# The merge of eight work queues in three causal attentions: from a greedy plan with a clock of its own to a written-out string for each

## What is computed

```python
# sublayer 6; sublayers 0 and 4 mask before the softmax instead
scores = jnp.einsum('bthd,bshd->bhts', q, k)
scores = scores * mask
attn = jax.nn.softmax(scores / T ** 0.5, axis=-1)
out = jnp.einsum('bhts,bshd->bthd', attn, v).reshape(B, T, H * Dh)
return out @ Wo
...
x = _layernorm(x + _L0_attn_ref(x, ...), axis=-1)      # 0, attention
x = _layernorm(x + _L0_ffn_ref(x, ...), axis=-1)       # 1, gated feed-forward
x = _layernorm(x + _L1_attn_ref(x, ...), axis=-1)      # 2, windowed attention
x = _layernorm(x + _L1_ffn_ref(x, ...), axis=-1)       # 3, mixture of experts
x = _layernorm(x + _L2_attn_ref(x, ...), axis=-1)      # 4, attention
x = _layernorm(x + _L2_ffn_ref(x, ...), axis=-1)       # 5, one matrix with binary weights
x = _layernorm(x + _L3_attn_ref(x, ...), axis=-1)      # 6, attention
x = _layernorm(x + _L3_ffn_ref(x, ...), axis=-1)       # 7, gated, ternary weights
```

## Time and profile before

| | us |
|---|---|
| runs: median of 3 (lowest to highest) | 1041.98 (1037.92 to 1046.48) |
| the profiled execution, its own time | 1044.26 |
| its span, first to last instruction | 1042.5 |
| TensorE busy | 972.7 (93%) |
| VectorE busy | 695.9 (67%) |
| ScalarE busy | 531.3 (51%) |
| GpSimd busy | 334.6 (32%) |
| mean granted TensorE clock | 0.984 |

### The profile page before, as it was taken

How to read it: one execution, slowest core, us unless ns; L and a number is a source line. 1 busy time by engine, 2 the same in 40 slices (tenths; PEclk the granted TensorE clock), 3 DMA queues, 4 the chain that set the end, 5 groups by cost and what they waited for, 6 DMA issues and landing times. The chain is left out here.

```text
span 1042.5 us, 16974 instructions
## 1 busy us (share of the span) xinstructions
PE 972.7 (93%) x6102; PEld 549.8 (53%) x6102; DVE 695.9 (67%) x1987; ACT 531.3 (51%) x1140; POOL 334.6 (32%) x465
## 2 busy tenths in 40 slices
PE   8999999989999999999999999999999988889896
PEld 3544454676454564443487544445555444445585
DVE  2677774686797987453223467777772778877587
ACT  4566665433879881121102456665544535665442
POOL 4211112233578871000001121112211256672452
PEclk9999999999999999999999899999999989999999
DMA  6000000100000200210000011000000000000001
GB/s 257 2 1 1 2 1 2 56 1 2 8 20 19 123 2 1 107 44 0 1 1 1 1 74 48 2 1 2 1 1 1 1 1 2 1 2 1 2 1 41
DMA packets 4823, 21.64 MB, mean 21 GB/s; under 512 B 489, under 2 KB 1769, under 8 KB 3844
## 3 DMA queue, kind: packets, MB, share of 16 engines
q1 hardware_dynamic: 4740, 20.55, 5.2%
HBM read 19.01 MB, written 1.05 MB: 19 GB/s over the span
## 5 line engine op out<-in xcount | busy, mean ns | idle before, releaser
L1000 ACT ACTIVATE PB<-pair 128x1024 f32<-128x1024 f32 (+3 forms) x288 | 223.2, 811 | 134.1 <-PE pair L1789 132.8
L1260 DVE CUSTOM_DVE_ANT_0 junk<-bank,cst 128x128 bf16<-128x128 f32 (+3 forms) x384 | 171.1, 488 | 106.4 <-PE bank L1773 104.4
L831 POOL TENSOR_SCALAR_AFFINE_SELECT PB<-PB 128x256 f32<-128x256 f32 x192 | 78.6, 412 | 308.1 <-ACT PB L1000 306.6
L1263 DVE TENSOR_REDUCE pmx<-bank 128x1 f32<-128x512 f32 x192 | 122.5, 685 | 40.9 <-PE bank L1773 40.2
L1773 PE MATMUL bank<-KO_r,QO_r 64*128 64x512 f32 (+3 forms) x576 | 139.7, 411 | 6.6 <-DVE pmx L1260 2.3
L1807 PE MATMUL pvb<-PB,V 128*32 128x512 f32 (+3 forms) x1152 | 122.7, 497 | 10.8 <-ACT PB L1000 8.8
L1785 PE MATMUL pair<-QO_r,KO_r 64*128 64x512 f32 (+3 forms) x576 | 114.7, 389 | 12.6 <-ACT PB L1000 10.8
L1773 PEld LDWEIGHTS bank<-KO_r,QO_r 64*128 64x128 f32 x576 | 72.1, 186 | 102.2 <-DVE pmx L1260 40.8
L837 POOL TENSOR_TENSOR parts_r<-y_f,parts_r 128x512 fp32r<-128x512 f32 x24 | 30.9, 1287 | 276.0 <-ACT parts_r L971 276.0
L1789 PE MATMUL pair<-ms,sel_r 64*128 64x512 f32 (+3 forms) x576 | 101.1, 344 | 0.0
L1071 ACT ACTIVATE KO<-pair,nm 128x128 f32<-128x128 f32 x256 | 90.1, 392 | 9.8 <-DVE nm L1487 9.4
(11 more groups left out here) (237 smaller groups left out, 1701.5 us busy)
## 6 DMA issues: line engine op xcount, KB each, us to landing
WF<-in_moe_gu SPq DMA_DIRECT2D x1, 3520.0 KB, 12.2
WF<-in_tern_w SPq DMA_DIRECT2D x1, 3072.0 KB, 10.6
WA<-in_w_att SPq DMA_DIRECT2D x2, 1024.0 KB, 10.5
V<-in_moe_d SPq DMA_DIRECT2D x1, 1792.0 KB, 7.4
xT<-in_xT SPq DMA_DIRECT2D x2, 512.0 KB, 5.9
WA<-in_w_att SPq DMA_DIRECT2D x2, 512.0 KB, 7.5
X<-in_x SPq DMA_DIRECT2D x1, 1024.0 KB, 10.8
A<-in_rope SPq DMA_DIRECT2D x1, 1024.0 KB, 4.8
```

Source lines behind the costliest of these rows:

```text
L831: pool.affine_select(p2, p2, pattern=[[0, 2], [1, P]], compare_op=ALU.is_ge, fill=0.0, base=0, channel_multiplier=-1).then_inc(causal, 1)
L1000: act.activation(pb[:, st % 2, 2 * i:2 * i + 2, 0:n], ps[:, :, 0:n], ACT.Exp, scale=scale)\
L1260: r_done(dve.tensor_tensor_reduce(junk[:, (r_used - 1) % 3, 0:n], ps[:, 0:n], tri[:, HALF - n:HALF], 1.0, LOWEST, ALU.add, ALU.max, accum_ ...
L1263: r_done(dve.tensor_reduce(to, ps[:, 0:n], AX.X, ALU.max))
```

## The change

The ranks, the `Clock` and all rules of what may start are taken out. For each of the three attentions a string gives the order in which the eight queues are popped. The queues, their inner order, the items and what each engine issues for an item stay the same, as do the waits. `acc` still follows a stage's last pv, and `norm` the last proj; the `weights` and `late` items go in behind the same items as before.

```diff
-LEAN = 600
-
-
-class Clock:
...
+ORDER = {
+    0: "BBBBBUBUUBUBUBUUBBUUBUBUBUBUTUBXUXUXUBUBUBUXPUXBUBUBPUXBUUBUBUTPUXXUXUBUPXXUAXUPUXXUPUBXUXUPUXXUPXUU"
...
 def attention_plan(s):
...
-    turns, accs, out, extra = [], [], [], []
...
-        now = [f for f in found if f[0] <= clock.pe + 30]
-        queue = min(now, key=lambda f: f[1])[2] if now else min(found, key=lambda f: f[:2])[2]
-        issue(queue.pop(0))
+    out = [("outT",)] + [("proj", k) for k in range(TH)] + [("new",)]
+    if SUBLAYERS[s + 1] == BIN:
+        out += [("bin", k) for k in range(TH)] + [("bin_new",)]
+    queues = {"B": operands(s, first, second), "U": [u for stage in units for u in stage],
+              "T": [("mT",) + stage for stage in STAGES], "X": [("exp",) + step + (i,) for step in STEPS for i in range(TWO)],
+              "P": [("pv",) + step for step in STEPS], "A": [("accT",) + stage for stage in STAGES], "O": out,
+              "E": [("suffix", t) for t in reversed(range(NT))] if s == LAST_ATT else []}
+    behind = {("pv", g, qh, TH * (qh + 1) - 1): ("acc", g, qh) for g, qh in STAGES}
+    behind.update({("proj", TH - 1): ("norm",), ("bin", TH - 1): ("bin_norm",)})
+    plan = []
+    for queue in ORDER[s]:
+        plan.append(queues[queue].pop(0))
+        if plan[-1] in behind:
+            plan.append(behind[plan[-1]])
```

More of the change, by code:

```diff
@@ L251, in attention_plan @@
[L251 to L332, removed]
@@ L394, in attention_plan @@
-    while build or units or exps or pvs or turns or accs or out:
-        while units and units[0][0] == "m":
-            issue(units.pop(0))
-        found = []
-        for rank, queue in ((-9000, turns), (-200, pvs), (-500, accs), (-400, out), (-300, extra), (None, exps),
-                            (None, units), (800, build)):
-            if queue:
-                at = ready(queue[0])
-                if at is not None:
-                    if rank is None:
-                        rank = (clock.act if queue is exps else clock.dve - LEAN) - max(clock.pe, at)
-                    found.append([at, rank, queue])
-        if build and found[-1][2] is build:
-            need = [x for x in wanted(units[0]) if x[0] == "s"] if units else []
-            late = [("v", pvs[0][3] // 2)] if all(("exp",) + pvs[0][1:] + (i,) in done for i in range(TWO)) else []
-            if any(x not in done for x in need + late):
-                found[-1][1] = -1000
-        now = [f for f in found if f[0] <= clock.pe + 30]
-        queue = min(now, key=lambda f: f[1])[2] if now else min(found, key=lambda f: f[:2])[2]
-        issue(queue.pop(0))
+    out = [("outT",)] + [("proj", k) for k in range(TH)] + [("new",)]
@@ L414, in attention_plan @@
+    behind = {("pv", g, qh, TH * (qh + 1) - 1): ("acc", g, qh) for g, qh in STAGES}
[5 more added lines that the diff above has]
+            plan.append(behind[plan[-1]])
+    assert not any(queues.values())
     if BIN in SUBLAYERS[s - 1:s]:
@@ L417, in attention_plan @@
     if s == 4:
-        for n, behind in ((0, ("norm",)), (1, ("new",)), (2, ("accT",) + STAGES[-2]), (3, ("weights", 2)),
-                          (4, ("accT",) + STAGES[-1])):
-            plan.insert(plan.index(behind) + 1, ("weights", n))
+        for n, item in ((0, ("norm",)), (1, ("new",)), (2, ("accT",) + STAGES[-2]), (3, ("weights", 2)),
+                        (4, ("accT",) + STAGES[-1])):
+            plan.insert(plan.index(item) + 1, ("weights", n))
     return plan
```

87 lines of the change are left out of this document (11 added, 76 removed).

## The result

The changed kernel takes 1024.40 us (median of 4 runs, 1021.98 to 1031.87); the kernel before, beside it, 1044.23. The ratio is 0.9842, 95% interval 0.9802 to 0.9883, so the gain is 16.5 us (12 to 21) where 31 were forecast; the two medians alone are 19.8 apart. The direction was right and the time lies in the range, but the gain came out a third to a half smaller than forecast.

The account below looks back on a forecast made before the run. No engine was taken as full; each waits in turn for another in a fixed order. Gains of 10.5 (sublayer 0), 10.9 (4) and 11.7 (6) less 2.0 sum to 31.1 us: 1013.2, predicted as 1011 us, range 990 to 1033.

Parts of the forecast that it names:

- the clock: Start of stage (0,1), sublayer 6: exps between maxima remove half the low-clock cost, 1.2 us gained (bounds 0 and 2.5).
- The pv items, sublayer 0: 20 fewer pvs closely behind their exp, 0.40 us each: 8.0 us; with exps and zeros 10.5.
- The pv items, sublayer 4: 21 fewer pvs closely behind their exp, 0.40 us each: 8.4 us; with exps and zeros 10.9.
- What is put in the way: Later weight sums in sublayer 4 lose 0.5 us, late `new` transposes 0.5 in each of three attentions: 2.0 together.
- The exps and zeros: Sublayers 0 and 4: 1.8 us less waiting for `pair` buffers, 0.75 for one group of zeros fewer; 2.5 each.
- Sublayer 6: Full stages 4.5 us, limited by GpSimd, other pvs 2.0, front 4.0, clock 1.2: 11.7 us gained.
- the 4.0: Front of sublayer 6: suffix items spread into stage (0,1)'s waits, against six maxima in a row; 4.0 us net gain.
- main case: The forecast's own terms hold, 31.1 us gained, time 1011 us, own range 997 to 1027; chance 0.61.
- first rival: The wait moves: exps then wait for `pair` or maxima for `bank`; 11 us gained, 1031 us; chance 0.18.
- `PB` with two tiles: Rival, all three attentions: exps wait for late pvs to free a `PB` tile; 15 us slower, 1057; chance 0.04.

Follow-up runs that it names:

- Removing both waits: Changed kernel with sublayer 4's last two weight sums earlier in VectorE's queue and three GpSimd ternary operations of sublayer 6's stage (3,1) moved: 1016.76 us, ratio 0.9727.
- the earlier sums: Changed kernel with VectorE's last two weight sums of sublayer 4 moved three and two accT items forward in its queue: 1017.26 us, ratio 0.976.
- Sublayer 0 alone: Only sublayer 0 in the new order, sublayers 4 and 6 in the old one as in the kernel before: 1032.76 us, ratio 0.9885.

## Why the prediction was right in direction and wrong in size

At equal clock the change gains 1047.0 - 1019.6 = 27.4 us, against 29.9 in the forecast, which is its 31.1 without the 1.2 that it gave to the clock. As run, 1044.5 - 1024.2 = 20.3 (means of 52 and 10 runs). The difference, 7.1 us, is the clock: 0.9829 before, 0.9747 after, times 8.7 us. So of the 10.8 us by which the gain falls short, 8.3 are the clock and 2.5 the schedule, in which larger misses of both signs cancel in part.

- *The step that failed: the clock.* The forecast booked one gain, 1.2 us in sublayer 6, and let the rest stand. It measured as a loss of 7.1. The stretch that it priced was read as 844 to 849 us; by the windows of the trace before it is at 0.50 from 840 on, and 838 to 840 reads 0.66. It is gone, as forecast, but others came. Two of them stand at the two new waits: the one at the accT in all eight profiles with this string and the sums in their old place (3.4 us in seven, 6.8 in one), the one at GpSimd's in all seven that have that wait (6.8 us in three, 3.4 in four), and none in a profile without it. At 0.42 us for each at the lower clock (last section) they are worth 1.4 and 1.4 to 2.9 us, so they leave part of the 7.1 open. Removing both waits raised the clock to 0.9812, but it was the earlier sums that did most of it, and with them another stretch went too: the 13.6 us of low clock at the front of sublayer 6. That one stood in five of seven profiles with new strings for 4 and 6 and the sums in their old place. It was 3.4 us in all five with the sums earlier, in three of them with 10.2 some 25 us later, and the same with sublayer 6 alone in the new order. So the run of six maxima is not enough for it, and what brings it stays open. Sublayer 0 alone has 0.9796, which may be chance in five runs.
- *The pv items, sublayer 0.* Right in the full stages: (2,1) and (3,1) have 10 such pvs fewer, at 0.40 us 4.0, and fell by 1.8 and 2.2 us, VectorE's work unchanged. The sublayer gained 10.8 us in the first trace, 12.8 in another, 10.5 less 0.5 forecast. That the whole fits is in part luck: its tail has 7 such pvs fewer, priced at 2.8, and gained 6.2, more than these and the 1.3 us of exps' waits gone there explain, while stage (1,1) lost 0.4.
- *The pv items, sublayer 4.* 10.9 forecast, 6.9 measured at equal clock. The full stages have 9 such pvs fewer, priced at 3.6, and gained 2.5 and 1.3 us. The tail has 8 fewer, priced at 3.2, and gained 0.6. There VectorE's queue is the bound: in both places that its sums had in it TensorE waits 3.0 to 3.4 us, and the tail takes 66.5. Its share alone would not say so, for 51 of 66 us is no more than its 18.55 of 22.27 in a stage of sublayer 0 that did gain. The same price was put on pvs where another engine was the bound.
- *What is put in the way.* 0.5 us was taken for the sums behind the last accT, with a bound of 2. It is 3.4, and the low clock comes on top. The margin of 1.25 us in the earlier trace rows was read; that accT moved behind two pvs and two pairs of exps was read too. The duration of these, over 4 us, was not set against the margin: from one accT to the last lay 7.63 us before and 3.38 after, 4.25 less with 1.25 to spare. The 3.0 that this gives is nearly the wait.
- *The exps and zeros.* The exps' wait in sublayer 0 fell by 2.0 of 2.3 us, where 1.8 was forecast.
- *Sublayer 6.* 11.7 forecast, 1.2 of it clock, 8.5 at equal clock. GpSimd was expected to hold the full stages at 22.5 to 23 us, a gain of 4.5. They stayed at 24.0 and 24.4; with stage (1,1) the three take 72.2 us instead of 72.6. GpSimd alone was not it: from 830.56 to 902.73 a pv waits for it once, 0.4 us. It does hold the first diagonal pv of stage (3,1) for 2.8 us, one wait with a low clock behind it. The prediction took the earlier trace rows for the limit of every full stage. The front gained more than the 4.0: from the end of sublayer 4 to `m` (0,1) 86.7 us before, 80.1 with sublayer 6 alone in the new order.
- *The rivals.* The wait moved in sublayer 4's tail and in sublayer 6, not in sublayer 0 (TensorE's waits for `bank` there come to 1.1 us before and 1.3 after); so the truth lies between the main case and the first rival. `PB` with two tiles never bound: no exponential's wait for a pv appears.

## What to carry to other kernels

Price a removed wait stage by stage, and only where no other engine's queue waits just behind it; that engine's share of busy time does not tell. An item moved near the end of a sublayer is to be held against the slack of what is queued behind it on the other engines. With a new wait of 3 us on TensorE, expect also a low clock behind it: here all 15 such waits had one. A wait that is gone from one row may have moved to another, so compare the length of the whole stretch too. When the mean clock differs between two kernels, compare them at equal clock before looking for lost microseconds in the schedule.

## What the hardware showed

The same program's mean granted clock varied between 0.973 and 0.992 in 52 runs, and its time with it, from 1053 to 1038 us. A microsecond at the lower clock costs some 0.42 (8.7 us for 0.01, which is 0.01 x 1025 x 2 = 20.5 us at 0.50), a little less than the half that the two levels would give if TensorE alone set the time. The places of the low stretches shift from run to run: with sublayer 4 in the old order, 602 to 612 us was low in one profile and nothing past 590 in another. And behind the wait of 2.8 us in sublayer 6 (2.6 in one profile), with TensorE busy 15.4 of the 16 us ahead of it in the first profile, 1.2 GHz stood for 3.4 or 6.8 us in seven profiles of seven.
